# A linear attention stage rewritten from outer products to masked score matrices, and powers split into four and 28 columns in every stage

## The reference, cut to what matters

```python
def _L1_attn_ref(x, Wproj, bproj, W0, ln_g, ln_b, gn_g, gn_b, Wout, bout):
    ...                                     # 16 heads of 8 features
    Z = jnp.einsum('bhsd,de->bhse', k, W0)
    y1, vjp1 = jax.vjp(ln_f, Z)
    dz1 = vjp1(y1 - v)[0]
    KK = mask * jnp.einsum('bhtd,bhsd->bhts', k, k)
    Z2 = Z - jnp.einsum('bhts,bhsd->bhtd', KK, dz1)
    y2, vjp2 = jax.vjp(ln_f, Z2)
    dz2 = vjp2(y2 - v)[0]
    A = mask * jnp.einsum('bhtd,bhsd->bhts', q, k)
    ctx = jnp.einsum('bhsd,de->bhse', q, W0) - jnp.einsum('bhts,bhsd->bhtd', A, dz1 + dz2)
    ...                                     # norm over tokens and features of a head
    return ctx @ Wout + bout

x = x + _L1_attn_ref(_layernorm(x), ...)
```

## Time and profile before

| | |
|---|---|
| median of 3 runs | 4256.7 us (4251.28 to 4260.63) |
| the profiled execution, its own time | 4255.34 us |
| its span in the trace | 4253.5 us |
| mean granted clock of TensorE in it | 0.848 of full speed |
| TensorE (PE) busy | 3267.3 us, 77% |
| VectorE (DVE) busy | 2784.9 us, 65% |
| ScalarE (ACT) busy | 1811.6 us, 43% |
| GpSimd (POOL) busy | 732.6 us, 17% |

### The profile page before, as it was taken

How to read it: one execution, slowest core, us unless ns; L and a number is a source line. 1 busy time by engine, 2 the same in 40 slices (tenths; PEclk the granted TensorE clock), 3 DMA queues, 4 the chain that set the end, 5 groups by cost and what they waited for, 6 DMA issues and landing times. The chain is left out here.

```text
span 4253.5 us, 71152 instructions
## 1 busy us (share of the span) xinstructions
PE 3267.3 (77%) x22808; PEld 2400.0 (56%) x22809; DVE 2784.9 (65%) x8181; ACT 1811.6 (43%) x5219; POOL 732.6 (17%) x947
## 2 busy tenths in 40 slices
PE   2668469467664888587778867999799997886897
PEld 2545259422222665475556654666577776665786
DVE  6546643489996777247885544555477775557997
ACT  1346334111111665234775433222155553445886
POOL 0045533200001677443000210000100000000000
PEclk9889579778886666588886777999899998998999
DMA  4040057300003100334000012333200000000000
GB/s 120 1 171 0 28 170 234 120 0 0 0 0 109 53 0 1 91 124 109 0 0 0 1 39 63 101 100 100 73 1 0 0 0 4 0 0 16 1 0 20
DMA packets 135738, 197.08 MB, mean 46 GB/s; under 512 B 24858, under 2 KB 90840, under 8 KB 133846
## 3 DMA queue, kind: packets, MB, share of 16 engines
q1 hardware_dynamic: 124078, 186.31, 14.0%
q0 software_dynamic: 11520, 9.05, 0.7%
HBM read 151.49 MB, written 58.63 MB: 49 GB/s over the span
## 5 line engine op out<-in xcount | busy, mean ns | idle before, releaser
L95 POOL TENSOR_TENSOR rstd<-vareps,minus_half 128x32 f32<-128x32 f32 x10 | 54.4, 5442 | 1179.7 <-DVE vareps L86 1155.9
L2622 ACT ACTIVATE l_ffn_sg<-l_ffn_p_g 128x512 f32<-128x512 f32 x168 | 100.4, 598 | 355.0 <-PE l_ffn_p_g L2659 355.0
L2593 DVE TENSOR_TENSOR l_ffn_part<-l_ffn_sg,l_ffn_share 128x512 f32<-128x512 f32 x168 | 116.3, 692 | 190.5 <-ACT l_ffn_sg L2622 189.1
L1278 PE MATMUL l_attn_p_s<-l_attn_outer,l_attn_upper 128*128 128x512 f32 x256 | 166.9, 813 | 75.5 <-DVE l_attn_outer L1221 58.8
L2649 PEld LDWEIGHTS l_ffn_p_o<-l_ffn_wd,l_ffn_h 128*128 128x128 f32 x1344 | 175.7, 191 | 85.0 <-issue 76.0
L1442 POOL DMA_INDIRECT slots_in<-l_xattn_x,l_xattn_slot x192 | 190.3, 991 | 81.9 <-issue 49.8
L2769 ACT ACTIVATE l_attn_E<-l_attn_p_s,l_attn_nm 128x128 f32<-128x128 f32 x512 | 181.3, 386 | 2.9 <-DVE l_attn_nm L2727 2.9
L2649 PE MATMUL l_ffn_p_o<-l_ffn_wd,l_ffn_h 128*128 128x128 f32 x1344 | 178.0, 275 | 2.3 <-DVE l_ffn_h L2596 1.6
L2659 PE MATMUL l_ffn_p_g<-l_ffn_f_xTall,l_ffn_wg 128*128 (+1 forms) x336 | 173.6, 599 | 0.5 <-DVE l_ffn_turned L2584 0.5
L2661 PE MATMUL l_ffn_p_u<-l_ffn_f_xTall,l_ffn_wu 128*128 (+1 forms) x336 | 172.5, 595 | 0.0
L1278 PEld LDWEIGHTS l_attn_p_s<-l_attn_outer,l_attn_upper 128*128 128x128 f32 x256 | 64.0, 262 | 164.8 <-issue 131.1
(11 more groups left out here) (813 smaller groups left out, 9503.3 us busy)
## 6 DMA issues: line engine op xcount, KB each, us to landing
l_experts_w<-in_L_ffn_w SPq DMA_DIRECT2D x72, 512.0 KB
l_ffn_share<-share_rows SPq DMA_DIRECT2D x112, 256.0 KB, 3.1
slots_in<-l_xattn_empty SPq DMA_DIRECT2D x8, 2145.0 KB, 24.1
shares_out<-l_xattn_zero SPq DMA_DIRECT2D x24, 512.0 KB, 10.5
l_out_got<-shares_out SPq DMA_DIRECT2D x16, 768.0 KB, 4.5
l_attn_toep<-kernel_rows SPq DMA_DIRECT2D x1, 8192.0 KB, 31.3
xattn_toep<-ssm_rows SPq DMA_DIRECT2D x1, 8192.0 KB, 31.7
l_slots_w<-in_L_ffn_w SPq DMA_DIRECT2D x32, 176.0 KB
```

Of the source, the lines that this page charges most:

```text
L1278: mm = pe.matmul(p_s[:, r, a], upper[:], outer[:, r, a * 512:(a + 1) * 512], start=True, stop=True)
L2593: dve.tensor_tensor(part[:, w], sg[:, w], share[:, slot], ALU.mult).then_inc(s.share_used, 1)
L2622: act.activation(sg[:, k], p_g[:, k], ACT.Silu).then_inc(s.silu_ready, 1)
```

## The change

**The second self attention.** TensorE projects k and q a second time with features on the partitions (`p_y`). ScalarE makes from this kT and eight copies `kqTm` of 128x256, each with all but every fourth head set to zero (by the new input `head4` as scale and `bhead` as bias). `scored` is then four matmuls, one for each group of 32 partitions (four heads), over 512 columns, which give the scores of 16 heads, 128x2048, in the four banks of `p_s`; it is done four times a pair: keys and queries, for two items. VectorE multiplies each with the triangle into SBUF (`masked_keys` L1204, `masked` L1200). dz1 and dz2 are written spread out, with zeros between the heads (`own`), and `applied` is now TensorE's, 32 matmuls with 32 output partitions; ScalarE copies the result (`sT1`, `sT2`), TensorE transposes it back (`rows_of`), and VectorE subtracts it from PSUM. Every part of the loop is in a new order with a depth of 4. The projection has 384 columns for 640. `kept_warm` and its input are gone. One load and two memsets are added; the stage has 48 semaphores for 39, and `l1_xattn` 50 for 47.

**The roots.** The power is done in two parts, four columns and 28 (`roots_first`, `roots_rest`); where the second part stands differs by stage: behind the first at once, or in POOL's turn 1 or 2 of the loop. VectorE's `norm_vector` becomes `norm_begin`, `norm_first` and `norm_rest`; the last stands at once behind or in a turn of the loop (3 in `l0_xattn`, `l0_route`, `l3_xattn`, 2 in `l3_attn`). Memsets and other work move between `norm_begin` and `norm_first`: in `l0_attn` `norm_begin` stands ahead of the wait for the loads, and with it POOL's power ahead of the tables that VectorE makes; in `l0_xattn` and `l3_xattn` a 128x2048 memset of `va` goes there. In `l2_film` the scales and the mask go ahead of `v2`. In `l1_xattn` the tokens come in two loads behind the others, on semaphores of their own; mask and second root are split too. `l3_attn` has both powers split. In `l2_ffn` the loop over groups of four items is written out, with `norm_rest` in the second group.

```diff
+FIRST = 4
+
+
+def norm_begin(R, dve, s):
     dve.tensor_scalar(R.vareps[:], R.stats[:, :, 1], EPS, None, ALU.add).then_inc(s.var_ready, 1)
+
+
+def norm_first(R, dve, s):
+
     dve.wait_ge(s.rstd_ready, 1)
-    dve.scalar_tensor_tensor(out=R.shift[:], in0=R.stats[:, :, 0], scalar=-1.0, in1=R.rstd[:],
+    dve.scalar_tensor_tensor(out=R.shift[:, 0:FIRST], in0=R.stats[:, 0:FIRST, 0], scalar=-1.0, in1=R.rstd[:, 0:FIRST],
                              op0=ALU.mult, op1=ALU.mult).then_inc(s.shift_ready, 1)
     dve.wait_ge(s.shift_ready, 1)
...
+def norm_rest(R, dve, s):
+
+    dve.wait_ge(s.rstd_ready, 2)
+    dve.scalar_tensor_tensor(out=R.shift[:, FIRST:], in0=R.stats[:, FIRST:, 0], scalar=-1.0, in1=R.rstd[:, FIRST:],
+                             op0=ALU.mult, op1=ALU.mult).then_inc(s.shift_ready, 1)
+    dve.wait_ge(s.shift_ready, 2)
+
+
+def roots_first(R, pool, s):
     pool.wait_ge(s.var_ready, 1)
-    pool.tensor_tensor(R.rstd[:], R.vareps[:], R.minus_half[:], ALU.pow).then_inc(s.rstd_ready, 1)
+    pool.tensor_tensor(R.rstd[:, 0:FIRST], R.vareps[:, 0:FIRST], R.minus_half[:, 0:FIRST], ALU.pow).then_inc(s.rstd_ready, 1)
+
+
+def roots_rest(R, pool, s):
+    pool.tensor_tensor(R.rstd[:, FIRST:], R.vareps[:, FIRST:], R.minus_half[:, FIRST:], ALU.pow).then_inc(s.rstd_ready, 1)
...
+                    if t == 1:
+                        roots_rest(R, pool, s)
...
+        kT, kqTm = sb("kT", [P, 2, W]), sb("kqTm", [P, 2, 2, 2, SUB, P])
+        proj = sb("proj", [P, PER, 3, 2, P])
+        keys, queries = sb("keys", [P, 2, H, P]), sb("queries", [P, 2, 2, H, P])
...
+        p_s, p_x, p_y, p_z, p_w = ps("p_s", [P, 4, 512]), ps("p_x", [P, 512]), ps("p_y", [P, 512]), ps("p_z", [P, 512]), ps("p_w", [P, 512])
...
+        def own(t):
+
+            return t[:, :, ::SUB + 1]
+
+        def spread(t):
+            return t.rearrange("p (a m) -> p a m", m=SUB).unsqueeze(3).broadcast_to((P, 8, SUB, HD))
+
+        causal = upper[:].unsqueeze(1).broadcast_to((P, H, P))
+        scores = p_s[:].rearrange("p j (m t) -> p (j m) t", m=SUB)
...
-                def applied(psum, b, read, part, x, step):
-
-                    for r in range(2):
-                        dve.wait_ge(psum, b * 2 + (r + 1))
-                        dve.tensor_tensor(square(part[:, r]), square(p_s[:, r].rearrange("p a n -> p (a n)")),
-                                          over_columns(x[:, r * P:(r + 1) * P]), ALU.mult).then_inc(read, 1)
-                    dve.wait_ge(read, b * 2 + 2)
-                    chain(dve.tensor_reduce(step, part[:].rearrange("p r (m i) -> p (r m) i", i=HD), AX.X, ALU.add))
-
-                for item in skewed(dve, 3, PAIRS):
+                def masked(b, u, r):
+                    dve.wait_ge(s.scores2_psum, b * 2 + (r + 1))
+                    dve.tensor_tensor(queries[:, u % 2, r], scores, causal, ALU.mult).then_inc(s.queries_ready, 1)
+
+                def masked_keys(b, r):
+                    dve.wait_ge(s.scores1_psum, b * 2 + (r + 1))
+                    dve.tensor_tensor(keys[:, r], scores, causal, ALU.mult).then_inc(s.keys_ready, 1)
+
+                for item in skewed(dve, 4, PAIRS):
...
+                        dve.tensor_tensor(own(dz1[:, u % 2]), apart(d1[:]), spread(st1[:, 1]), ALU.mult).then_inc(s.dz1_ready, 1)
...
+                        act.activation(kT[:, u % 2], p_y[:, 0:W], ACT.Identity, bias=bqk[:, 0:1])
+                        for c in range(2):
+                            for m in range(SUB):
+                                last = act.activation(kqTm[:, u % 2, c, :, m], side(p_y[:, c * W:(c + 1) * W]), ACT.Identity,
+                                                      scale=head4[:, m:m + 1], bias=bhead[:, c, m:m + 1])
+                        last.then_inc(s.kq_ready, 1)
...
+                def scored(u, r, c):
+                    for j in range(4):
+                        rows = slice(32 * j, 32 * j + 32)
+                        mm = pe.matmul(p_s[:, j], kT[rows, u % 2, r * P:(r + 1) * P], kqTm[rows, u % 2, c, r].rearrange("p m t -> p (m t)"), start=True, stop=True)
+                    return mm
...
+                def applied(out, a, dz):
+                    for r in range(2):
+                        for m in range(SUB):
+                            for j in range(4):
+                                mm = pe.matmul(out[32 * j:32 * j + 32, r * P:(r + 1) * P], dz[:, 4 * r + j, SUB * m:SUB * (m + 1)].rearrange("p n e -> p (n e)"),
+                                               a[:, r, SUB * j + m], start=(m == 0), stop=(m == SUB - 1))
+                    return mm
...
+                sp.dma_start(ctxt[:, 0:FIRST], A["ctx_tokens"][:, 0:FIRST]).then_inc(s.tokens_in, DMA)
+                sp.dma_start(ctxt[:, FIRST:], A["ctx_tokens"][:, FIRST:]).then_inc(s.others_in, DMA)
...
+                for t, item in enumerate(written_out(9)):
+                    if t == 1:
+                        roots_rest(R, pool, s)
+                    if t == 2:
+                        pool.wait_ge(s.var2_ready, 2)
+                        pool.tensor_tensor(var2[:, FIRST:], var2[:, FIRST:], R.minus_half[:, FIRST:], ALU.pow).then_inc(s.rstd2_ready, 1)
...
+                    if t == 1:
+                        dve.tensor_scalar(mneg[:, FIRST:], m4[:, FIRST:].bitcast(U8), 1.0, 1e30, ALU.subtract, ALU.mult).then_inc(s.mask_ready, 1)
+                    if t == 2:
+                        dve.wait_ge(s.rstd_ready, 2)
+                        squared(FIRST, NB)
+                    if t == 3:
+                        dve.wait_ge(s.rstd2_ready, 2)
+                        composed(FIRST, NB)
...
+                    if k == 2:
+                        norm_rest(R, dve, s)
+                        squared(FIRST, NB)
+                    if k == 5:
+                        dve.wait_ge(s.rms_ready, 2)
+                        scaled(FIRST, NB)
```

464 lines of the change are left out of this document (257 added, 207 removed).

## The result

The changed kernel takes 4223.4 us (median of 4 runs, 4222.8 to 4223.8) where the one before takes 4258.7 (median of the 4 runs beside it): a ratio of 0.9918, 95% interval 0.9904 to 0.9932. It is faster by 35 us. Forecast were 63 us less, 4193, with a range of 4168 to 4230.

A forecast was written before the change was run, and what follows sets the result against it. VectorE was taken to bound `l1_attn`. From the profiled 4255.3 us, -41.5 for the new second self attention and -22 for the split roots gave 4191.8, stated as 4193 against the median, range 4168 to 4230.

The forecast's parts named there:

- VectorE's work in a turn: `l1_attn` loop: 14.0 us a turn removed from VectorE, 9.3 added by four 128x2048 multiplications, so 29.8 becomes 25.1.
- TensorE's prices: `l1_attn`: at full clock 1.16 us a call of `scored`, 2.1 of `applied`; at half clock 2.3 and up to 4.2.
- ScalarE ... beside VectorE's first gradient: no cost: `l1_attn`: ScalarE's eight masked copies with kT take 4.7 us, 11 a turn in all, at no cost.
- a sign against itself: `l1_attn`, profile after: the prediction expected that ScalarE would not be waited for; no size given.
- I take 1.2 us a turn: `l1_attn`: VectorE's wait ahead of `masked_keys(b, 1)`, from half clock on TensorE, makes the turn 26.3 us.
- rival (a): `l1_attn`: the clock stays at half for more of the turn; a turn of 28.5 us, total 4227; chance 0.15.
- 16 x (26.3 - 29.8): `l1_attn`: the gain of a turn, 29.8 to 26.3 us, counted for all 16 turns.
- Fill, drain, prologue: `l1_attn` outside steady turns: +12 us for first and last turns, +1.9 prologue, +0.6 semaphores.
- part 1: The new second self attention, `l1_attn`: turns, fill, drain, prologue and semaphores together, -41.5 us.
- Part 2: The roots taken apart in all stages that normalise: -22 us, bounds -12 and -27.
- rival (d): Split roots give little: slow 28-column powers hold up POOL and loads replace the power; -8 us, total 4207; chance 0.12.
- -5.2, and the stage's VectorE chain moves with it: `l0_attn`: early roots remove VectorE's 5.56 us stand before the shift, less some 0.4; later VectorE work moves equally.

The follow-up runs named there:

- applied_first: Changed kernel with TensorE's projection in `l1_attn` moved behind the scores of the second item's queries: 4203.3 us, ratio 0.9877.
- warm_second: Changed kernel with twelve bf16 matmuls without use ahead of TensorE's wait for dz2 in `l1_attn`: 4217.4 us, ratio 0.9917.
- roots_only: Changed kernel with the old `l1_attn`, its root in two parts one behind the other: 4239.5 us, ratio 0.9962.
- whole_root: Changed kernel with the power of `l0_attn` in one piece of 32 columns, still early: 4212.2 us, ratio 0.9897.
- both_warm: Changed kernel, projection behind second item's query scores, twelve matmuls without use ahead of dz2, six ahead of dz1: 4184.3 us, ratio 0.9829.

## Why the prediction was right or wrong

**The sign and the bound** were right: VectorE sets the pace of `l1_attn`, its work fell by what the rows said, and the time lies in the range, in the part given to rivals, 30 us above the forecast. That it lies there is in part luck: neither ScalarE's copies in TensorE's list nor the slow loop in `l0_attn`, which took it there, is among the rivals.

**VectorE's work in a turn: right.** Forecast -4.7 us, measured -5.1. The 2048-wide products were 2.29 us, as costed.

**TensorE's prices: right.** `scored` took 1.14 (1.16 forecast) and 2.06 to 2.46 at the half clock (2.3); `applied` 1.95 (2.1) and 3.64 (up to 4.2). The forms cost nothing beyond this; what drained for a change of form, if anything, is in them.

**"ScalarE ... beside VectorE's first gradient: no cost": wrong, and it is the dearest step.** ScalarE's copies are hidden from VectorE, but TensorE waits for them (1.8 us a turn) with the first application queued behind that wait. I asked only whether ScalarE would be done before VectorE needed it, not what stood behind the wait in TensorE's list. `applied_first` puts it at 17 us of stage time. The price itself was not too low: ScalarE was busy for 9.1 us of a turn, for 11 forecast. The profile after shows what the prediction had named as a sign against itself, TensorE waiting for L1286.

**"I take 1.2 us a turn": mis-sized only a little.** It was 1.5, from the clock, as argued: `warm_second` took it away. The reason given, the idle time just ahead, is only part of it, since behind 1.8 idle us the application was as slow. And `warm_second` shows that such a wait can't be priced alone, since it came back at the next hand-over. The turn was 27.3, at the edge of the 25.7 to 27.3 that the forecast called its own and short of rival (a), 28.5.

**"16 x (26.3 - 29.8)": wrong count.** A steady turn's gain was taken for all 16. The start of the first gradient's last product (L1229, L1231) shows it: before, 16 of them from 860.8 to 1299.6; after, from 871.1 to 1280.4. That is 438.8 and 409.3 us for 15 turns, of which the first three, not yet full, gained 0.6 us together, and the other twelve 28.9. By the forecast's own turn, twelve would have been -42, not -56.

**Fill, drain, prologue: +14.5 forecast.** The sum came near, the split did not: of it 7 were for one more draining turn, which cost nothing. The way to the first gradient grew by 12.0 us, the drain by 0.0 (46.2 in both); the first three turns take 0.6 off: +11.4. Together: 12 x -2.41 + 11.4 = -17.5, the measured difference. Of the 24 us missing in part 1, 14 are the count (4 x 3.5), 13 the smaller gain of a turn (12 x 1.1), less 3 for the cheaper fill.

**Part 2: -22 forecast, -14.5 measured** by the spans (18.7 less by the medians of `roots_only`). Most stages came as reckoned: `l3_attn` -5.9 for -6.5, `l2_ffn` -3.7 for -2, both cross attentions at the ends -2.9 and -3.8 for -1.5 and -2.5. In `l3_attn` the first transpose came 8.2 us after the first load and not 7: it waited for the last of the loads, `gamma`, and not for `wqkv`. In `l1_xattn` the first 7-column power came 5.0 us earlier in the stage, with both 28-column powers ahead of it, as the order had shown (forecast 4.2); the stage as a whole gave 1.6 and in `roots_only` 4.1, both within what it varies by:

```profile
1339.29 4.80 POOL L113 TENSOR_TENSOR rstd<-vareps,minus_half 128x28 f32<-128x28 f32 x1
1344.83 4.80 POOL L1486 TENSOR_TENSOR l_xattn_var<-l_xattn_var,minus_half 128x28 f32<-128x28 f32 x1 [0.74 <-DVE l_xattn_var L1527]
1349.58 1.48 POOL L1492 TENSOR_TENSOR l_xattn_rms<-l_xattn_ssq,minus_half 128x7 f32<-128x7 f32 x1
```

The 28 columns took 4.80 and the four 1.04 us on average, so rival (d), slow powers, fell. The step that failed is `l0_attn`: "-5.2, and the stage's VectorE chain moves with it". The shift did come 5.8 us sooner in the stage, and 7 us were lost in a loop whose text the change did not touch. With `whole_root` the stage gives -4.5. The prediction took it without saying so that a loop whose text stays keeps its pace.

**Not forecast at all:** that the 18 matmuls without use were worth 15 us of stage time (9 of the whole) in the kernel before. I had counted their removal as time that TensorE saves. In the new loop the two places with 18 such matmuls are worth 18 us of stage time (from `applied_first`, 487.2, to `both_warm`, 469.1).

## What to carry to other kernels

When work is given to an idle engine, look for the engine that waits for it and read on in that one's list: the instruction that costs is the one queued behind the wait, and moving it past may be free. A single buffer handed back and forth several times a turn can turn a wait removed at one hand-over into one at the next: here one removal gave 17 us, another by itself nothing clear of noise, and that one paid only with the others. And multiply a steady turn's gain by the steady turns only, with fill and drain compared by the same landmark in both traces.

## What the runs showed of the hardware

- The same 64 matmuls took 3.64 us behind 3.9 idle us and behind 1.8, and 1.95 behind twelve matmuls without use. Behind a pause of 2.9 us at the loop's end the scores took 2.42 us, behind one of 2.04 in another turn 1.14.
- Matmuls without use paid where the next real ones are waited for: 1.47 us of them ahead of the first application gave 10 us of stage time (479.3 to 469.1).
- A loop of one vector instruction ran at 0.493 or at 0.715 us a turn with nothing changed in it: fast in the traces of six kernels (149 VectorE instructions ahead), slow in those of eight (151 or 153). It costs 7 us here and shows as a gap that ends on issue. The added 0.1 us stands ahead of the branch with 151 instructions ahead and two instructions earlier with 153, so it keeps its place in the code; why, stays open.
